# First mixture of experts rebuilt: score rows broadcast onto the transposed input, shared expert ahead of the routed ones, all copies of y on VectorE

## What is computed

```python
x = x + _L0_ffn_ref(_layernorm(x), gate, expert_bias, w1, w2, w3, shared_w1, shared_w2, shared_w3)

xt = x.reshape(-1, 256)                                  # 2048 rows
scores = sigmoid(xt @ gate.T)                            # 8 experts
_, sel = top_k(scores + expert_bias, 2)                  # bias only for the choice
# for each expert e and each row that chose it:
xb = (xt * score_of_e[:, None]).astype(bfloat16)         # the score scales the input
h = silu(xb @ w1e.T) * (xb @ w3e.T)                      # bfloat16 products, hidden size 128
out_r += h @ w2e.T
# the shared expert, for every row, in float32:
hs = silu(xt @ shared_w1.T) * (xt @ shared_w3.T)
out = hs @ shared_w2.T + out_r
```

## Time and profile before

| | us |
|---|---|
| median of 3 executions | 3052.1 (3050.13 to 3052.7) |
| the profiled execution, its own time | 3052.09 |
| its span, first to last instruction | 3050.3 |
| changed block up to the choice of experts, 2448 to 2484 | 36 |
| changed block, four groups of nine steps, 2484 to 2634 | 150 |

### The profile page before, as it was taken

One profiled execution on the slowest core, in us unless ns is written; L12 is line 12 of the kernel. 1 busy time (PEld: TensorE's weight loads), 2 busy tenths in 40 slices (PEclk: granted clock), 3 DMA queues, 4 the chain that ended last, 5 costly groups with the idle time before them and its releaser, 6 DMA issues. The chain is left out here.

```text
span 3050.3 us, 58797 instructions
## 1 busy us (share of the span) xinstructions
PE 2872.9 (94%) x18706; PEld 2455.7 (81%) x18733; DVE 2123.1 (70%) x4543; ACT 2003.6 (66%) x4930; POOL 1692.9 (56%) x2119
## 2 busy tenths in 40 slices
PE   7989999799999999999999999999999977599798
PEld 5768888688888888888888888888888954388655
DVE  7975444677777777777777777777777768766544
ACT  5656666677777777777777777777777647566211
POOL 6766664466556556556555655655655344466132
PEclk9999999999999999999999999999999979799799
DMA  5456767311111111111111111111111010253510
GB/s 180 135 156 207 207 206 230 126 54 54 41 68 54 41 68 54 41 66 43 53 42 66 54 41 68 54 41 67 50 44 41 1 48 1 87 167 122 177 42 27
DMA packets 249668, 253.38 MB, mean 83 GB/s; under 512 B 12471, under 2 KB 225600, under 8 KB 249377
## 3 DMA queue, kind: packets, MB, share of 16 engines
q1 hardware_dynamic: 229856, 228.92, 22.7%
q10 hardware_dynamic: 17312, 15.73, 1.8%
q0 software_dynamic: 2208, 5.12, 0.6%
HBM read 165.71 MB, written 84.93 MB: 82 GB/s over the span
## 5 line engine op out<-in xcount | busy, mean ns | idle before, releaser
L1027 ACT ACTIVATE w_hi<-ps_t 128x512 fp32r<-128x512 f32 (+2 forms) x1024 | 570.0, 557 | 415.1 <-PE ps_t L1267 411.7
L1097 DVE TENSOR_REDUCE piece_max<-ps_s 128x1 f32<-128x512 f32 (+2 forms) x1024 | 631.3, 622 | 257.5 <-PE ps_s L1254 229.6
L1123 DVE TENSOR_TENSOR w_lo<-ps_t,w_hi 128x512 fp32r<-128x512 f32 (+2 forms) x1024 | 656.1, 641 | 200.4 <-ACT w_hi L1027 183.8
L1287 PE MATMUL ps_o<-w_hi,v_hi 128*128 128x256 f32 (+1 forms) x1856 | 595.8, 321 | 0.0
L1194 POOL TENSOR_SCALAR prob<-prob,inv_sum 128x512 f32<-128x512 f32 (+2 forms) x768 | 477.5, 641 | 195.6 <-DVE inv_sum L1113 195.6
L1289 PE MATMUL ps_o<-w_hi,v_lo 128*128 128x256 f32 (+1 forms) x1856 | 523.4, 282 | 0.0
L1288 PE MATMUL ps_o<-w_lo,v_hi 128*128 128x256 f32 (+1 forms) x1856 | 522.2, 281 | 0.0
L1015 ACT ACTIVATE prob<-ps_s,neg_max 128x512 f32<-128x512 f32 (+2 forms) x768 | 487.4, 635 | 43.8 <-DVE neg_max L1104 35.2
L1267 PE MATMUL ps_t<-ident,prob 128*128 128x128 f32 (+1 forms) x2784 | 515.9, 272 | 0.0
L1249 PE MATMUL ps_s<-k_hi,q_hi 128*128 128x512 f32 (+2 forms) x1024 | 403.6, 394 | 27.5 <-ACT prob L1015 18.2
L1267 PEld LDWEIGHTS ps_t<-ident,prob 128*128 128x128 f32 (+1 forms) x2784 | 359.5, 140 | 52.3 <-issue 0.2
(11 more groups left out here) (289 smaller groups left out, 6258.1 us busy)
## 6 DMA issues: line engine op xcount, KB each, us to landing
v_scratch<-v_out SPq DMA_DIRECT2D x120, 256.0 KB, 3.0
raw_k<-k_scratch SPq DMA_DIRECT2D x32, 960.0 KB, 6.9
raw_v<-v_scratch SPq DMA_DIRECT2D x32, 960.0 KB, 4.7
k_scratch<-k_out SPq DMA_DIRECT2D x104, 256.0 KB, 2.7
q_scratch<-out_t SPq DMA_DIRECT2D x64, 256.0 KB, 2.5
r_all<-r_scratch SPq DMA_DIRECT2D x32, 512.0 KB, 4.1
raw_q<-q_scratch SPq DMA_DIRECT2D x32, 512.0 KB, 5.1
first_prob<-in_ctx_t ACTq DMA_DIRECT2D x50, 256.0 KB, 2.8
```

Of the source, the lines that this page charges most:

```text
L1027: nc.scalar.activation(pt_hi[keys, k % RING, cols], ps_t[keys, k % 2, cols], ACT.Copy).then_inc(hi_done, 1)
L1097: nc.vector.tensor_reduce(piece_max[:, n % 2, p:p + 1], ps_s[:, p, lo - p * PC:hi - p * PC], AX.X, ALU.max).then_inc(max_ready, 1)
L1123: nc.vector.tensor_tensor(pt_lo[keys, k % RING, cols], ps_t[keys, k % 2, cols], pt_hi[keys, k % RING, cols].bitcast(F32), ALU.subtract).th ...
L1287: nc.tensor.matmul(out, v_hi[gi][keys, vs], pt_hi[keys, k % RING, cols], start=blk == (0 if qt else 1), stop=False)
```

## The change

The scores no longer scale rows before they are turned. VectorE writes the weights as [P, E0, NT], TensorE turns this 128x128 array once, ScalarE copies it to `weight4_t`, one DMA writes it to `score_scratch` in DRAM, and 32 DMAs (one for each group and expert) read a row of 512 scores back, broadcast to all 128 partitions, into `weight4_all`. GpSimd then multiplies `xt` by such a row (two products of 128x512 for a step, L1460 of the changed kernel) straight into `xbt`, which now has four buffers. The turns of `xb` on TensorE and the copies of `ps_b` on ScalarE are gone.

The shared expert of all four groups is computed ahead of the routed steps, its silu as (1 + tanh(h/2)) * h * 0.5 straight from PSUM. `ps_h3` has two banks. TensorE makes the hidden products three steps ahead. The hardware loop is gone: all 32 routed steps are written out. All copies of y, also those of a group's last expert, are on VectorE: `of_act` is False throughout, so `copy_y` of ScalarE is never called.

```diff
+                sp.wait_ge(weight_copied, 1)
+                sp.dma_start(score_dram, weight_t[:, :]).then_inc(weight_written, 16)
+                sp.wait_ge(weight_written, 16)
+                for i in range(NG):
+                    for e in range(E0):
+                        if i:
+                            sp.wait_ge(row_loaded[e], 16 * i)
+                        rows = score_dram[e * NT + i * GT:e * NT + (i + 1) * GT, :].rearrange("(a t) n -> a (t n)", a=1)
+                        sp.dma_start(weight_all[:, e, i * N:(i + 1) * N], rows.to_broadcast([P, N])).then_inc(row_loaded[e], 16)
...
-                def scale(i, e):
-                    if positive(i * E0 + e - 1):
-                        pool.wait_ge(xbt_ready, i * E0 + e - 1)
-                    for t in range(GT):
-                        tile = i * GT + t
-                        nc.gpsimd.tensor_scalar(xb[:, e % 2, t, :], xn[:, tile, :], weight[:, tile, e:e + 1], 1.0,
-                                                ALU.mult, ALU.mult).then_inc(xb_ready, 1)
+                def inputs(k):
+                    i, e = divmod(k, E0)
+                    pool.wait_ge(row_loaded[e], 16 * (i + 1))
+                    if k >= 4:
+                        pool.wait_ge(h3_ready, SHARED + k - 3)
+                    cols = slice(i * N, (i + 1) * N)
+                    for c in range(DC):
+                        nc.gpsimd.tensor_tensor(xbt[:, k % 4, c, :], xt[:, c, cols], weight_all[:, e, cols], ALU.mult).then_inc(xbt_ready, 1)
...
+                half_tanh(0)
+                half_tanh(1)
+                act.wait_ge(weight_turned, 1)
+                nc.scalar.activation(weight_t[:, :], ps_weight, ACT.Copy).then_inc(weight_copied, 1)
+                half_tanh(2)
+                half_tanh(3)
+                nc.scalar.preload_act_table_set("natural_log_exp_and_others")
+                for k in range(2):
+                    exponential(k)
+                    copy_h3(k)
+                for k in range(STEPS0):
+                    inverse(k)
+                    if k + 2 < STEPS0:
+                        exponential(k + 2)
+                        copy_h3(k + 2)
...
+                def copy_y(k, h):
+                    dve.wait_ge(y_done, 2 * k + h + 1)
+                    if k:
+                        dve.wait_ge(summed, 2 * (k - 1) + h + 1)
+                    nc.vector.tensor_copy(y_bf[:, h, :], ps_y[:, h, :]).then_inc(y_by_dve, 1)
...
+                for k in range(STEPS0):
+                    if k + 2 < STEPS0:
+                        copy_h1(k + 2)
+                    if k + 1 < STEPS0:
+                        denominator(k + 1)
+                    if k % E0 == 1 and k > E0:
+                        add_x(k // E0 - 1)
+                    if k:
+                        copies_of_y(k - 1)
+                    silu(k)
+                    gated(k)
+                copies_of_y(STEPS0 - 1)
                 add_x(NG - 1)
...
+                hidden(0)
+                hidden(1)
+                pe.wait_ge(weighted, 1)
+                nc.tensor.transpose(ps_weight, weight[:, :, :].rearrange("p e t -> p (e t)"), ident[:, :]).then_inc(weight_turned, 1)
+                hidden(2)
+                hidden(3)
+                shared_outputs(0)
...
+                for k in range(STEPS0):
+                    if k + 3 < STEPS0:
+                        hidden(SHARED + k + 3)
+                    if k % E0 == 1 and k > E0:
+                        shared_outputs(k // E0)
+                    outputs(k)
+                    if k:
+                        sums(k - 1)
```

More of the change, by code:

```diff
@@ L1414, in moe_two_of_eight, with y_copied @@
+        def y_copied(k, h):
+            done = [(a, b) for a in range(k + 1) for b in range(2) if (a, b) <= (k, h) and of_act(a, b) == of_act(k, h)]
+            return (y_by_act if of_act(k, h) else y_by_dve), len(done)
         with nc.Block() as block:
@@ L1459, in _ @@
                 act.wait_ge(logits, 1)
[L1460 to L1467, removed]
@@ L1500, in last_outputs @@
-                def last_outputs(i, h):
-                    k = (i * E0 + LASTS - 1) * 2 + h
-                    act.wait_ge(y_done, k + 1)
-                    act.wait_ge(summed, k - 1)
-                    nc.scalar.activation(y_bf[:, h, :], ps_y[:, h, :], ACT.Copy).then_inc(y_last_copied, 1)
-                def group(i, last):
-                    for s in range(STEPS):
-                        if s:
-                            inverse(i, s)
-                        elif positive(i):
-                            last_outputs(i - 1, 0)
-                            last_outputs(i - 1, 1)
-                        if s + 1 < E0:
-                            inputs(i, s + 1)
-                        elif s == LASTS and not last:
-                            inputs(i + 1, 0)
-                        if s < LASTS:
-                            exponential(i, s + 1)
-                            copy_h3(i, s + 1)
-                        elif not last:
-                            exponential(i + 1, 0)
-                            copy_h3(i + 1, 0)
@@ L1525, in _, with half_tanh @@
-                inputs(0, 0)
-                exponential(0, 0)
-                copy_h3(0, 0)
-                group(0, False)
-                with act.Fori(1, NG - 1) as i:
-                    group(i, False)
-                group(NG - 1, True)
-                last_outputs(NG - 1, 0)
-                last_outputs(NG - 1, 1)
+                nc.scalar.activation(score_exp[:, :, :], ps_logits.rearrange("p (t e) -> p t e", t=NT), ACT.Exp, scale=-1.0).then_inc(score_exps, 1)
+                def half_tanh(j):
+                    act.wait_ge(h1_ready, j + 1)
+                    if j >= 2:
+                        act.wait_ge(siluf_ready, j - 1)
+                    nc.scalar.activation(tanh[:, j % 2, :], ps_h1[:, j % 2, :], ACT.Tanh, scale=0.5).then_inc(tanh_ready, 1)
@@ L1535, in _ @@
+                if of_act(STEPS0 - 1, 1):
+                    copy_y(STEPS0 - 1, 1)
             @block.vector
@@ L1563, in add_x, with copies_of_y @@
+                def copies_of_y(k):
+                    for h in range(2):
+                        if not of_act(k, h):
+                            copy_y(k, h)
                 def add_x(i):
@@ L1716, in hidden @@
+                            last = nc.tensor.matmul(ps[:, n % 2, :], a, b, start=c == 0, stop=c == DC - 1)
                         last.then_inc(done, 1)
@@ new lines, in outputs @@
+                def outputs(k):
+                    pe.wait_ge(act_ready, k + 1)
+                    for h in range(2):
+                        if k:
+                            pe.wait_ge(*y_copied(k - 1, h))
+                        for t in range(2):
+                            last = nc.tensor.matmul(ps_y[:, h, t * D:t * D + D], act_bf[:, k % 2, (2 * h + t) * P:(2 * h + t + 1) * P],
+                                                    w_bf[:, 2, k % E0, :], start=True, stop=True)
+                        last.then_inc(y_done, 1)
@@ L1776, in _, with sums @@
+                def sums(k):
+                    for h in range(2):
+                        pe.wait_ge(*y_copied(k, h))
+                        for t in range(2):
+                            last = add(2 * h + t, ident_bf[:, :], y_bf[:, h, t * D:t * D + D], last=k % E0 == E0 - 1)
+                        last.then_inc(summed, 1)
                 pe.wait_ge(gate_loaded, 32)
```

330 lines of the change are left out of this document (118 added, 212 removed).

## The result

| | before | after |
|---|---|---|
| median of 12 executions each | 3052.39 (3050.13 to 3057.37) | 3059.05 (3056.85 to 3067.01) |
| profiled execution, its own time | 3052.09 | 3058.71 |
| its span | 3050.3 | 3056.9 |
| end of the changed block | 2633.84 | 2639.91 |
| granted clock, mean of the span | 0.973 | 0.964 |

After/before is 1.0026 [1.0018, 1.0033]. The forecast was 3056 in 3035 to 3070. The profiled pair differs by 6.6 us, and 6.1 of them are there already at the end of the changed block (2633.84 to 2639.91), so the change costs where it was made.

The account below looks back on a forecast made before the run. No engine full: the groups are a ring of waits. First act ends 2499, plus 118.8 (27 steps of 4.4), 12.4 (four of 3.1), 3.9 additions and 3.8 tail gives 2637.9 against 2633.84, +4 us: 3056, range 3035 to 3070.

Parts of the forecast that it names:

- That products block VectorE: Routed steps: silu, act and den each wait for GpSimd's whole running product, making a step 4.6 to 5.1 us.
- the row at 37.54: First block, before trace: a VectorE instruction of 0.41 us takes 1.28 beside a 1.30 us GpSimd product, waiting it out.
- the silu row: Before trace: silu loses 0.18 us behind a scaling of half a microsecond; by this a step would be 3.6.
- they do not meet: Rival, chance 0.23: GpSimd's products fall under PSUM copies, or waits are short; step 3.6 to 3.7 us, time 3036.
- lower bound for a product: GpSimd product in a routed step: 0.69 us if as cheap per element as a scaling; 1.29 was taken.
- the two orders: Routed steps: GpSimd's product starts before silu (step 5.1 us) or silu goes first; mean 4.6 at full clock.
- The clock: Routed steps: TensorE falls to half clock at times, step about 4.0 us; rival of mostly half clock, chance 0.12, 3045.
- The two prices that were mixed for it: Routed step: 4.6 to 5.1 us at full clock and 4.0 at half clock, mixed to 4.4.
- 8 us of filling: Start of routed steps: filling the ring of four xbt buffers takes 8 us from 2491, first act ending at 2499.
- The head: Before the routed steps: write 2.4 us, first broadcast 3.2, first scores ready at 2488.4, first hidden product at 2491.0.
- Tail: End of the changed block, from the last act to its end: 3.8 us, against 3.6 before.
- the cases of no change and slower: Whole kernel: same, 3046.0 to 3058.2 us, chance 0.39; slower, above 3058.2, chance 0.31.

Follow-up runs that it names:

- e2: Changed kernel, but GpSimd starts a step's first product only after den and the second only after act: 3041.54 us, ratio 0.9967 to the kernel before.
- e7: Changed kernel, but VectorE makes den ahead of the h1 copy and both GpSimd products wait for den: 3038.21 us, ratio 0.9958 to the kernel before.
- e3: Changed kernel plus eight TensorE additions of zeros ahead of the outputs in most routed steps: 3064.06 us, ratio 1.0039 to the kernel before.
- e8: Changed kernel with the old input path (GpSimd scales rows, TensorE turns, ScalarE copies), one ps_h3 bank, h3 copied before Ln and Exp: 3032.4 us, ratio 0.9931.
- e6: Changed kernel, but xt and the scores are rounded to bfloat16 ahead of GpSimd's products: 3055.11 us, ratio 1.0008 to the kernel before.

## Why the prediction was right, step by step

**That products block VectorE** was the step on which all hung, and it held. The product was read off a row of 80 products in another block at 1.29; it takes 1.27 alone and 1.34 on average, its own waiting included. Beside a product silu takes 1.08 to 1.51, act 1.37 to 1.40 and den 0.75 to 1.34, by how much of the product is left, as the row at 37.54 had said, and not 0.18 more, as the silu row by itself suggested. The trace agrees with the rule of the Trainium skill ("SBUF — State Buffer", Who interferes with whom) that the two exclude one another for a whole instruction; in e2, which places them apart, act takes 0.42 and a product 1.27. The rival "they do not meet" (3036, steps of 3.6 to 3.7) is what e2 and e7 come near: 3041.54 and 3038.21, steps of 3.67 and 3.61. The prediction's lower bound for a product, 0.69 "were it as cheap per element as a scaling", doesn't follow from its row: two scalings of 538 ns for as many elements are 1.08. The sum didn't use it.

**That the two orders alternate** held as well, though not one by one: steps of 5.06, 4.64, 4.02 and 3.70 stand beside each other. GpSimd starts 0.14 behind the end of the hidden products here (2566.11 + 1.03 to 2567.28); I had read 0.20. Silu comes 0.29 after it. The step without the x additions is 4.46 on average over 25 steps (115.3 us from 2499.56 to 2614.88, less 3.9); I took 4.4 for 27.

**The clock** was wrong in size and in what it does to a step. Of the steps from 2500 to 2612 nearly half ran at the lower of the two levels (0.77 granted is 0.46 of the time at 1.2 GHz), where I had said "at times" and had given that state as the bulk of the steps 0.12. And a step at the lower level was to take about 4.0. The windows view, asked from act to act, gives this for the 22 of the 25 steps that hold no x addition:

| granted clock of the step | steps | mean us | from, to |
|---|---|---|---|
| 0.91 to 1.00 | 6 | 4.73 | 4.12, 5.06 |
| 0.65 to 0.84 | 10 | 4.15 | 3.70, 4.71 |
| 0.50 to 0.56 | 6 | 4.87 | 4.64, 5.32 |

The steps that lie almost wholly at the lower level take 4.64 and more; the shortest are steps in which the level changes. A step of 5.06 and one of 3.70, each from act to act:

```profile
2578.77:2583.83 5.06, 2.46 (x15) 1.24 (x13) 4.84 (x6) 2.26 (x4) 2.66 (x3) 1.00 0.00 0
2587.85:2591.55 3.70, 2.60 (x11) 1.48 (x12) 3.33 (x6) 2.54 (x5) 3.23 (x3) 0.72 0.00 0
```

The mean of the steps came to 4.46 for 4.4 all the same. The two prices that were mixed for it, 4.6 to 5.1 and 4.0, were not both right, nor was the share of each, so that it came so near is partly luck.

In the first two steps the ring of four isn't full: GpSimd works without a pause, and nothing makes it late. Timeline of GpSimd there:

```profile
2495.43 17.25 POOL L1460 TENSOR_TENSOR xbt<-xt,weight_all 128x512 bf16<-128x512 f32 x13
```

Thirteen products in 17.25 us, at half clock (the row of 2498 to 2512 in the windows above), with silu, act and den blocked each time: two steps of 5.31, in this kernel and, to a hundredth, in e2, e3 and e7. The second of them in e3 has a granted clock of 1.00 and takes 5.32, so the length is that of the blocks and not of the clock. The prediction had this only inside "8 us of filling".

**The head** was right at its end and wrong within. Timeline from the turned weights to the first hidden product, and the page's row of the broadcasts (KB each, median us from issue to landing):

```profile
2482.71 0.34 SPq L1435 DMA_DIRECT2D score_scratch<-weight_t  x1
...
2484.26 7.10 SPq L1442 DMA_DIRECT2D weight_all<-score_scratch  x8
...
2488.07 3.73 POOL L1460 TENSOR_TENSOR xbt<-xt,weight_all 128x512 bf16<-128x512 f32 x3 [19.97 <-DMA weight_all<-score_scratch]
...
2491.05 0.38 PE L1687 MATMUL ps_h<-xbt,w_bf 128*128 128x512 bf16 x1
```

```profile
weight_all<-score_scratch SPq DMA_DIRECT2D x32, 256.0 KB, 9.6
```

The first product stands at 2488.07 for a forecast 2488.4, the first hidden one at 2491.05 for 2491.0. The write and its wait took 1.55 (2482.71 to 2484.26) where I had 2.4, the first broadcast 3.8 where I had 3.2: two misses that cancel. The 32 broadcasts take 9.6 us each at the median, not 2.4 to 4.1, and eight are issued within 7.1 us, so they are under way beside one another; the steps never waited for one. The first act ended at 2500.93, 1.9 later than forecast: filling the ring took 9.9 from 2491.05, not 8.

**The sum, term by term.** First act +1.9. From there to the end of the last act 134.1 for 135.1 forecast: 25 steps of 4.46 where 27 of 4.4 had been taken, then four of 3.07 (forecast 3.1) and two of 3.71. Tail 4.9 for 3.8: the granted clock from 2627.17 to 2640 is 0.51, and e3, with 1.00 in its last steps, has a tail of 4.1. The block's last instruction in the timeline of the changed kernel, for the earlier trace rows:

```profile
2638.62 1.29 DVE L1614 TENSOR_TENSOR x_sb<-ps_acc,x_sb 128x512 f32<-128x512 f32 x2 [0.70 <-PE ps_acc L1692]
```

Together 2639.91 for 2637.9: misses of +1.9, -1.0 and +1.1. That is 2.0 of the 2.7 us by which the median moved more than forecast (6.7 for 4); the rest is within the spread of the executions. The move lies on the line between the cases of no change and slower, 0.39 and 0.31; faster had 0.30, mostly by a rival in which GpSimd and VectorE do not meet, and e2 and e7 show that the places of the products keep the changed kernel from it.

**What I did not price:** that the change holds a gain and a loss of such size. I summed the new block as one and compared its end. e8 shows 21 us gained and 27 lost. Whether the 27 would be less with smaller pieces of product (four of 256 instead of two of 512) was not tried.

## What to carry to other kernels

An engine with slack is not free if its instructions hold up those of the busy engine: price a GpSimd instruction by what it holds up. Place such instructions by a semaphore behind the last instruction that they would block and ahead of those that read PSUM; that took 17 us off 25 steps here, with no work removed. Short ones cost less (silu and act beside scalings of 0.5 us paid 0.24 and 0.16 in e8, beside a product of 1.3 us up to 1.1), but a scaling differs from a product in more than its length. Where a large edit moves the time little, build it with each half undone before believing that it does little.

## What the runs showed of the hardware that I had not expected

A GpSimd product of 128x512 costs 1.34 us from float32 and 1.22 from bfloat16 with the waits (e6). A VectorE instruction that PSUM feeds is not slowed beside a product: 0.68 for a copy in every kernel here. In the steps with products a lower TensorE clock need not lengthen a step: leaving out the first two, those at 0.50 to 0.56 took 4.64 and 4.65, those at 1.00 4.12 to 5.06, and e3, which raised the clock of the steps from 0.77 to 0.86, was not faster. In the steps without products it does: 3.71 and 3.70 at the lower level, 3.07 at the upper. That the products hide it because GpSimd starts later behind slower hidden products is argued from the timelines; no run separates it. Nor did the clock fall by itself: with the products placed (e2, e7) it is 1.00 through the steps from 2518 to 2606.
